# A fused cross-attention and mixture-of-experts kernel: new prologue, new order of the work up to the experts, and W1 as the stationary side of the up product

## What is computed

```
q = layernorm(x) @ w_q                     # 16 heads of 64
k, v = split(context @ w_kv)
attn = softmax(q k^T / 8);  x = x + tanh(g0) * ((attn v) @ w_out + b_out)
xn = layernorm(x);  probs = softmax(xn @ Wr^T)        # 8 experts
top 2 of 8 experts per token, their weights normalised to 1
h = silu(xn @ W1[e]^T)                     # 1024 hidden
x = x + tanh(g1) * sum over the two e of gate[e] * (h @ W2[e]^T)
```

## Time and profile before

| what | us |
|---|---|
| runs, median (lowest to highest) | 638.88 (637.75 to 642.58) |
| the profiled execution, its own time | 636.74 |
| its span, first to last instruction | 635.0 |
| mean granted TensorE clock | 0.939 |
| PE busy (share of the span) | 510.4 (80%) |
| DVE, ACT, POOL busy | 398.1, 342.7, 267.6 |
| first product of the attention on PE | 47.37 |
| last residual row of the attention on DVE | 310.87 |
| start of the up product of tile 2 | 382.12 |

### The profile page before, as it was taken

How to read it: one execution, slowest core, us unless ns; L and a number is a source line. 1 busy time by engine, 2 the same in 40 slices (tenths; PEclk the granted TensorE clock), 3 DMA queues, 4 the chain that set the end, 5 groups by cost and what they waited for, 6 DMA issues and landing times.

```text
span 635.0 us, 15659 instructions
## 1 busy us (share of the span) xinstructions
PE 510.4 (80%) x5430; PEld 397.9 (63%) x5432; DVE 398.1 (63%) x943; ACT 342.7 (54%) x548; POOL 267.6 (42%) x295
## 2 busy tenths in 40 slices
PE   0009999999999999987510359999999999999981
PEld 0008878888888888866410137777777777777761
DVE  4986788888888999977599764242423333333330
ACT  0075888778786868773153344444444444444440
POOL 3000433537373837395338544343434343434320
PEclk9999999999999999979855579999999999999997
DMA  8801003131615141487800102323231323232311
GB/s 292 358 1 41 4 18 103 34 102 35 101 36 102 35 85 35 93 258 196 187 0 0 37 1 36 50 33 50 33 50 33 50 33 50 33 50 33 50 18 17
DMA packets 23669, 43.96 MB, mean 69 GB/s; under 512 B 4053, under 2 KB 19798, under 8 KB 21187
## 3 DMA queue, kind: packets, MB, share of 16 engines
q1 hardware_dynamic: 14498, 32.84, 18.6%
q0 software_dynamic: 8544, 10.30, 10.3%
q10 hardware_dynamic: 576, 0.14, 0.1%
HBM read 33.54 MB, written 9.73 MB: 68 GB/s over the span
## 4 chain that ended last, share of the span: by engine, by line
PE 72%; DMA 7%; DVE 7%; POOL 4%; issue 4%; ACT 3%; SPq 0%; POOLq 0%; ACTq 0%; DVEq 0%
PE j_bank L1329 34%; PE st_bank L1329 15%; PE st_bank L1498 4%; PE o_bank L1329 4%; PE max_bank L1478 3%; DMA table<-entry,slot 3%; PE o_bank L1600 3%; PE j_bank L1600 3%; PE j_bank L1391 2%; DVE amax L915 2%; DMA stage<-in_w 2%; DMA w1s<-in_x 2%; PE max_bank L1577 2%; POOL table L546 2%; DVE w2s L1121 1%
## 5 line engine op out<-in xcount | busy, mean ns | idle before, releaser
L525 POOL TENSOR_TENSOR pT<-pT 120x512 f16<-120x512 f32 x64 | 75.5, 1189 | 159.9 <-ACT pT L699 158.2
L626 POOL DMA_INDIRECT out<-yt,row_of x39 | 61.5, 1578 | 143.0 <-DVE yt L1294 143.0
L1329 PE MATMUL j_bank<-w2s,hT 128*128 x936 | 110.7, 276 | 6.6 <-DVE w2s L1121 4.7
L1329 PEld LDWEIGHTS j_bank<-w2s,hT 128*128 128x128 f16 x936 | 92.4, 99 | 27.0 <-issue 7.3
L1329 PE MATMUL st_bank<-w1s,xsT 128*128 x468 | 108.7, 382 | 0.5 <-DVE xsT L1277 0.5
L1294 DVE TENSOR_SCALAR yt<-j_bank,gate_y 128x256 f32<-128x256 f32 x39 | 18.9, 484 | 134.9 <-PE j_bank L1329 134.9
L853 ACT ACTIVATE hT<-o_bank,h_scale 128x512 f16<-128x512 f32 x39 | 26.8, 687 | 99.5 <-PE o_bank L1600 99.5
L1329 PEld LDWEIGHTS st_bank<-w1s,xsT 128*128 128x128 f16 x468 | 46.0, 98 | 48.8 <-issue 3.2
L847 ACT ACTIVATE hf<-st_bank,z_scale 128x512 f32<-128x512 f32 x78 | 53.4, 687 | 37.7 <-PE st_bank L1329 37.7
L698 ACT ACTIVATE pT<-st_bank,exp_bias,logit_scale 120x512 f32<-120x512 f32 x64 | 49.7, 777 | 7.8 <-PE st_bank L1501 7.1
L699 ACT ACTIVATE pT<-st_bank,exp_bias,logit_scale 120x512 f16<-120x512 f32 x64 | 49.9, 779 | 0.0
(11 more groups left out here) (212 smaller groups left out, 1003.8 us busy)
## 6 DMA issues: line engine op xcount, KB each, us to landing
stage<-in_w SPq DMA_DIRECT2D x10, 1024.0 KB, 10.0
w2s<-in_w SPq DMA_DIRECT2D x4, 1024.0 KB, 9.0
out<-x SPq DMA_DIRECT2D x17, 128.0 KB, 4.1
xin<-in_x SPq DMA_DIRECT2D x8, 256.0 KB, 3.3
w1s<-in_x SPq DMA_DIRECT2D x2, 1024.0 KB, 8.9
w1s<-in_wkv SPq DMA_DIRECT2D x1, 2048.0 KB, 13.3
xres<-in_x SPq DMA_DIRECT2D x16, 128.0 KB, 4.0
xn<-xn SPq DMA_DIRECT2D x16, 128.0 KB, 1.7
```

What stands on the lines that cost most here:

```text
L525: pool.tensor_tensor(pT[g % 2][:, 1, h, :], pT32[:, h, :], pT[g % 2][:, 0, h, :], ALU.subtract).then_inc(pT_low[h], 1)
L626: pool.indirect_dma_start(out=out[:], out_offset=bass.IndirectOffsetOnAxis(row_of[:, t:t + 1], 0), in_=yt[t % 2][:], in_offset=None, compu ...
L1329: ins = pe.matmul(out, lhs[i](a), rhs[i](c), start=(i == 0 and a + c == 0), stop=(i == n - 1 and a == 1))
```

## The change

The whole difference is a reworked kernel up to the tile loop and a reworked tile loop. Its parts:

1. Loads at the start: w_v, w_k, w_q, w_out, context, x of batch 0, the rest of x (two of 7 blocks), W1 of experts 0 and 1. The maxima are taken weight by weight, each with its own matmul (`attn_maxima`) and scale; only w_v and w_out share one. The splits go by halves (`PIECES`), partly on POOL (`weight_low`), and `norm_factors` moves to POOL, once for batch 0 alone.
2. The constants that the first product doesn't need are made later (`constants`).
3. W2 gets its bound early: each expert's W2 is loaded during the attention (8 more loads of 1 MB), ACT sums its magnitudes (`w2_sum`, in place of DVE's eight `w2_max`), and `w2_scale` is done by round 8. W2 is loaded a second time at the last batch, as before, and split then.
4. `scattered` becomes two semaphores by the parity of the batch, and `scatter` no longer waits for earlier ones on POOL. `route` waits for the batch before last instead.
5. Other orders of the rounds on all engines, out_product in two halves, the ends of the rounds stretched so that the W2 splits and the tables interleave; `y_scales` and `gate_y` are made before `tables_done`, all low parts on DVE too; silu's table is loaded ahead (`load_silu`).
6. Tile loop: SP copies W1 of the tile's expert (1 MB, 8 KB in each partition) from `w1s` into one of the four places `w1_tile` (the memory of `stage` and `land`). The up product has 128x128 blocks of it stationary and `xsT` (128 columns) moving: 48 matmuls, and its result has hidden units on the partitions. `hidden_T` is gone; ACT and DVE split `hf` from SBUF.

```diff
@@ the loads and the bounds
+            sp.dma_start(raw_v, wkv[:, :, INNER:2 * INNER]).then_inc(raw_in[3], 16)
+            sp.dma_start(raw_k, wkv[:, :, 0:INNER]).then_inc(raw_in[1], 16)
+            sp.dma_start(raw_q, wq).then_inc(raw_in[2], 16)
+            sp.dma_start(raw_o, wo).then_inc(raw_in[4], 16)
+            sp.dma_start(raw_ctx, ctxT).then_inc(raw_in[0], 16)
             sp.dma_start(xin[:], x_b[0]).then_inc(xin_in, 16)
-            for i in range(2):
-                sp.dma_start(x_all[i], x_v[:, 8 * i:8 * i + 8, :]).then_inc(x_all_in[i], 16)
...
+            def w2_sum(b, e):
...
+                act.wait_ge(w2_early_in[e % 2], 16 * (e // 2 + 1))
...
+                nc.scalar.activation(w1_part(E - 1, 1, 0, 2048), w2_early[e % 2], ACT.Abs,
+                                     accum_out=amc2[:, e:e + 1]).then_inc(w2_sum_done, 1)
@@ DVE, the order of the first rounds (p from -5), cut to the steps of the weights and statistics
+            for p in range(-5, B + 22):
+                weight_max(p + 5, 3)
...
+                constants(p + 5)
...
+                weight_max(p + 5, 1)
...
+                weight_max(p + 4, 4)
...
+                attn_scales(p + 4, 2)
+                weight_low(p, 4, 0)
...
+                weight_max(p + 5, 2)
...
+                attn_scales(p + 3, 3)
...
+                weight_max(p + 4, 0)
...
+                attn_scales(p + 3, 0)
+                weight_low(p + 1, 3, 0)
+                attn_scales(p + 5, 1)
...
+                weight_low(p + 3, 2, 0)
@@ POOL, the low part of a piece of a weight
+                chain.link(pool.tensor_scalar(raw, raw, up[:, i:i + 1], None, ALU.mult))
+                pool.tensor_tensor(half(i, 1, lo, hi), raw, half(i, 0, lo, hi), ALU.subtract).then_inc(w_low[i][j], 1)
@@ SP, behind the rounds
+            for t in range(TILES):
+                if t == 0:
+                    sp.wait_ge(tables_done, 1)
+                if t < 4:
+                    sp.wait_ge(w2_low[4 + t], 4)
+                else:
+                    sp.wait_ge(z_full, 2 * (t - 3))
+                e = sp.value_load(expert_of[0:1, t:t + 1], min_val=0, max_val=E - 1)
+                sp.dma_start(w1_tile[t % 4], w1s[:, bass.ds(e, 1)].rearrange("p e s k f -> p (e s) k f")).then_inc(w1_tile_in[t % 4], 16)
@@ ACT, one tile
+            def hidden(t, par, early):
                 for a in range(2):
...
                     later(z_full, t, a)
...
+                    nc.scalar.activation(hf[par][:, cols], z_bank[a][:], ACT.Silu,
                                          scale=z_scale[:, bass.ds(t, 1)]).then_inc(silu_done, 1)
...
+                    later(silu_done, t, a)
...
+                    nc.scalar.activation(hT[par][:, 0, 4 * a:4 * a + 4, :], hf[par][:, cols].rearrange("p (c n) -> p c n", c=4),
                                          ACT.Copy, scale=h_scale[:, bass.ds(t, 1)]).then_inc(h_high, 1)
@@ PE, one tile
-            def up_product(e, t, par, first):
+            def up_product(t, par, buf, before, first):
 
                 pe.wait_ge(xs_low, t + 1)
-                if not first:
-                    pe.wait_ge(silu_done, t * 2)
+                pe.wait_ge(w1_tile_in[buf], before * 16 + 16)
                 for a in range(2):
-                    three(z_bank[a][:], [lambda p, kc=kc: xsT[par][:, p, kc, :] for kc in range(KC)],
-                          [lambda p, kc=kc: w1s[:, bass.ds(e, 1), p, kc, 512 * a:512 * a + 512].rearrange("p e f -> p (e f)")
-                           for kc in range(KC)]).then_inc(z_full, 1)
-
-            def hidden_T(t, par, first):
...
+                    if not first:
+                        pe.wait_ge(silu_done, t * 2 + a - 1)
+                    for q in range(4):
+                        c = (4 * a + q) * P
+                        ins = three(z_bank[a][:, q * P:(q + 1) * P],
+                                    [lambda p, kc=kc: w1_tile[buf][:, p, kc, c:c + P] for kc in range(KC)],
+                                    [lambda p, kc=kc: xsT[par][:, p, kc, :] for kc in range(KC)])
+                    ins.then_inc(z_full, 1)
```

More of the change, by code:

```diff
@@ L861, in step @@
                     xs_part(t + 1, 1 - par, first)
-                if first:
-                    high2(5)
-                    high2(6)
-                silu(t, par)
-                h_split(t, par)
-                if first:
-                    high2(7)
+                hidden(t, par, isinstance(t, int) and t < 2)
             run_tiles(act, step)
@@ L919, in _, with constants, x_stats @@
-            ins.then_inc(diag4_done, 1)
+            def constants(b):
+                if b:
+                    return
+                dve.wait_ge(ident_done, IDENT)
+                nc.vector.tensor_copy(identb[:], ident[:]).then_inc(zero_done, 1)
+                chain.link(nc.vector.tensor_copy(base[0][:], seg[:]))
+            def x_stats(b, part):
+                if b:
+                    return
+                if part == 0:
+                    dve.wait_ge(xin_in, 16)
+                    src, t0, n, done = xin, 0, NT, stats0_done
+                else:
+                    dve.wait_ge(x_all_in[part - 1], 16)
+                    src, t0, n, done = x_rest[part - 1], NT + REST * (part - 1), REST, stats_done[part - 1]
+                for t in range(n):
+                    ins = nc.vector.bn_stats(stats[:, t0 + t, :], src[:, t, :])
+                chain.link(ins)
+                for t in range(n):
+                    ins = nc.vector.bn_aggr(mv[:, t0 + t, :], stats[:, t0 + t, :])
+                ins.then_inc(done, 1)
@@ L1271, in y_scales, with row_ids @@
                 chain.link(nc.vector.tensor_scalar(y8, y8, tg[:, 1:2], None, ALU.mult))
+                by_tile(count, z_scale)
+                by_tile(h8, h_scale)
                 by_tile(y8, y_scale)
-                chain.link(nc.vector.tensor_tensor(gate_y[:], gate_y[:], y_scale[:], ALU.mult))
+            def row_ids(b):
+                if b == B - 1:
+                    dve.wait_ge(found_T, 1)
+                    nc.vector.tensor_copy(row_of[:], j_bank[0][:, 0:TILES]).then_inc(rows_done, 1)
@@ L1275, in xs_rest @@
+            nc.vector.tensor_tensor(gate_y[:], j_bank[0][:, 64:64 + TILES], y_scale[:], ALU.mult).then_inc(tables_done, 1)
             def xs_rest(t, par):
```

960 lines of the change are left out of this document (551 added, 409 removed).

## The result

The changed kernel takes 618.26 us (median of 4 runs, 615.39 to 621.03) where the kernel before takes 638.36 beside it: a ratio of 0.967, 95% interval 0.962 to 0.973. It is faster by 20 us, not by the 58 that were forecast, and 618 lies outside the range of 564 to 604.

| stretch, us | before | forecast | after |
|---|---|---|---|
| prologue and attention, to R | 310.9 | 300.9 | 310.1 |
| the gap, R to up(2) | 71.2 | 53.7 | 64.9 |
| 36 tiles, up(2) to up(38) | 229.1 | 201.1 | 218.8 |
| the end, from up(38) | 23.8 | 20.8 | 22.8 |
| span | 635.0 | 576.5 | 616.6 |

The account below looks back on a forecast made before the run. DMA, VectorE's maxima, then splits bound the prologue; PE the attention and loop; VectorE and scatters the gap. Loop 28, end 3, prologue 10, gap 17.5: 636.7 - 58.5 = 578.2, with 2.1 for the median 580 us; range 564 to 604.

Parts of the forecast that it names:

- The pace: Tile loop, up product: 48 matmuls of 128 columns, each with its own weight load, at 56 ns, 2.68 us in all.
- Rival (b): Tile loop: sustained pace of 81 ns per matmul, tile 6.8, loop +15 in place of -28, kernel 623; chance 0.05.
- (a): Tile loop: the scatter becomes the bound, sharing DMA engines with the copy; cycle 6.1, kernel 598; chance 0.10.
- (c): Tile loop: a copy within SBUF outlasts a tile, PE waits for W1; 7.7 per copy, kernel 660; chance 0.03.
- Rival (d): Prologue and gap give nothing because dependencies across engines eat it, only the loop gains; kernel 607; chance 0.10.
- the gathers have two tiles of slack: Tile loop: the gathers were taken to have two tiles to spare, so no wait was added for them.
- the loop's own turn: Tile loop: 0.05 us per tile, the difference between 6.36 measured and 6.31 summed before, kept in the new 5.57.
- its sign: Tile loop: the forecast is wrong if PE's idle time there names a DMA; PE was expected busy above 99%.
- w2_sum ... I count 0: Attention: ACT's W2 sums add 8 x 2.1 where it has free time; counted 0, with +5 above for single PE stalls.
- norm2(7) ends at about 5.5: Gap: the last batch's second norm ends about 5.5 us after the last residual, having started at 3.9 before.
- route(7) at 13.4: Gap: the last batch's routing ends 13.4 us after the last residual, following logits at 10 and choose at 11.
- find_rows may wait for scatter(7) to land (8.3 after it, 27: hidden): Gap: the last scatter lands by 27, while POOL's low parts run to 28.6, so the row search loses nothing.

Follow-up runs that it names:

- e1: Changed kernel with GpSimd's gather in the tile loop issued one tile further ahead (t+4 in place of t+3): 611.66 us, 0.9612 of the kernel before.
- e7: e1 with the tile loop of TensorE, ScalarE and VectorE written out without a hardware loop: 594.89 us, 0.9380 of the kernel before.
- e9: Changed kernel with SyncE's first two early W2 loads ahead of the load of x for batch 2: 607.55 us, 0.9581 of the kernel before.
- e8: e1 with TensorE's second register load in each turn's first tile moved behind the up product: 601.32 us, 0.9485 of the kernel before.
- e3: e1 with only the first four copies of W1 made, so later tiles use wrong weights: 602.1 us in its one execution.
- e12: e10 with batch 5's scatters ahead of the last residual on GpSimd and one W2 low part behind the last scatter: 614.88 us, 0.9679.
- e16: Edits of e7, e9 and e12 together, first W1 copies let go at rows_done, the moved W2 low part made by VectorE: 583.21 us, 0.9215.
- e2: e1 with the hardware loop in 3 turns of 12 tiles instead of 9 turns of 4: 622.03 us, 0.9799 of the kernel before.
- e10: Changed kernel with reordered gap: last norm factors, W2 expert 5's high part, tile counts, row search, two W2 low parts behind first gathers: 612.32 us, 0.9665.

## Why the prediction was right and wrong

**The pace, right.** 56 ns for a matmul of 128 columns with its own weights, from a row of 120 columns, gave 2.68 for the up product; 2.68 was measured in 36 tiles, and the tile without stalls is 5.52 against the forecast 5.57. Rival (b) is out. The Trainium skill's sustained 81 ns ("TensorE: Matmul & The Clock Gate", section "Back-to-back issue gap") doesn't hold here; the measured 56 decides. The copies land in 4.5 to 5.1 in e1, e7 and e9 (4.7 forecast), the scatters in 3.8 to 4.1 (3.8). Rivals (a) and (c) are out: e7 has all this traffic and no idle PE. Rival (d) named the weak places but not their size: prologue, gap and loop each gave part.

**The loop, 18 short.** The step that failed is "the gathers have two tiles of slack". I counted the slack in buffers (four, one in use). But gather(t+3) stands in GpSimd's order behind scatter(t-1), which waits for the end of down(t-1), one tile before tile_T(t+3). In the old tile the eight transposes (0.88) lay between the end of the down product and the next tile's start, and the chain fitted. From the kernel before, a gather and the transposes of its rows:
```profile
600.80 0.99 POOL L606 DMA_INDIRECT xg<-xn,row_of  x1 [0.30 <-issue]
604.94 0.38 PE L1577 MATMUL max_bank<-ident,xg 128*128 128x128 f32 x2
```
With its 2.8 to landing it was there 1.3 early; in the new kernel it comes 0.3 to 1.3 late. The second failed step is the 0.05 for "the loop's own turn", carried over from before. In e8 the second register load alone, moved behind queued matmuls, is worth 5 to 6 us in nine turns; before, load and jump together had cost 0.2 a turn, with 12 long matmuls in the up product. That short instructions leave PE's queue too thin to cover it is my reading, not shown. Also open is why the turn costs 0.8 more with copies than without (e1 against e3), and what the jump costs alone. The forecast had named its sign: it was to be wrong if PE's idle time in the loop named a DMA, and it did.

**Prologue and attention, 9 short.** "w2_sum ... I count 0" failed, and not by its length of 2.1. I named "single stalls of PE behind it" and priced them at 5 at most, without asking when its data is requested: SyncE's order has the load of x for batch 2 in front, which waits for ScalarE. With that order changed (e9) the first norm_o is at 66.4, where 67 was forecast, and R at 302.0, where 301 was. The cause is shown, its share of the 9 is not: R of the unchanged kernel moves from 304.6 to 311.5 from set to set. The sign named for this stretch, that it ends later than 303, came true.

**The gap, 11 short.** "norm2(7) ends at about 5.5" and "route(7) at 13.4" took each step's duration and left out what stands ahead of it in GpSimd's and ScalarE's order. With these orders changed, routing ended at R+13.5 (e12) and the tables were done at R+38.9 (e16), the forecast 13.4 and 38. So the durations added up about right. What I left out on top is that the index buffer of the last routing waits for the scatters of two batches earlier. "find_rows may wait for scatter(7) to land (8.3 after it, 27: hidden)" held in the changed kernel (345.95, no wait) and was wrong once the rest was quick. Of the 11, 9 lie ahead of tables_done and 2 behind it: up(0) starts 5.7 after it (5.5 forecast), but from there to up(2) it takes 12.3 where 10.2 was forecast, 1.7 of it a wait ahead of the first turn that is gone in e8. Of the shorter gap (61.6 in e12, 57.0 in e16) little has shown in a total.

**The end, 2 short.** From up(38) to the last gated output it is 602.00 - 593.77 = 8.2 (8.0 forecast). The other 14.6 were 12.8 before (from 622.2). I had left out the last two scatters, one behind the other: the last waits 2.9 for the landing of the one before.

## What to carry to other kernels

When an engine gets faster, recompute each loop-carried chain around it from one issue to its use, through every queue it passes; buffers tell how far ahead a transfer may run, an engine's order tells how far it does. Two stalls that hide behind each other look worthless when removed singly (5.7 and 3.9 us here, 19.6 together), so test pairs. A stretch made of queue orders may give nothing until the last of its holders is gone, and the next may be a transfer that the others had covered. And where one stretch moves by several us from set to set, a total says little on a change of that size in another.

## What the hardware did unexpectedly

A hardware loop's body of 12 tiles costs 8 to 9 us per jump back (e2), with 26 instruction packets in 200 us, while one of 4 tiles has 3 packets and straight code has 24 and no stall at all (e7). The tile with one more register load on TensorE ahead of short matmuls takes 0.8 us more (e2, inside a turn); with the load behind 48 queued ones nine turns took 5 to 6 us less (e8). The last scatter of a row into the table lands 8 to 10 us after its issue though the DMA engines are nearly idle (share 0.06 from 306 to 334 us in e10); the median is 5.5.
